# A four-stage hybrid block on one NeuronCore: loads on one queue, layer norm beside the rounds, another order in power attention

## What is computed

```python
x = x + mamba(layernorm(x))     # selective scan: E = 256 channels, 16 states
x = x + ffn(layernorm(x))       # two layers of windowed attention (8 heads of 64) and gated FFN
x = x + power(layernorm(x))     # 16 heads of 8, P = (q.k)^2 with a decay, causal
x = x + ffn(layernorm(x))       # the same weights again

# power attention, per head
log_G = cumsum(log_sigmoid(x @ Wg))
Z = 2*log(abs(S) + 1e-7) + log(scale) + log_G[t] - log_G[s], masked causal
y = exp(Z - max) @ V / sum(exp(Z - max))
```

## Time and profile before

| | |
|---|---|
| runs, median of 3 | 3021.56 us (3019.85 to 3024.13) |
| profiled execution, its own time | 3025.83 us |
| span of its trace | 3024.0 us |
| granted TensorE clock, mean | 0.975 of 2.4 GHz |
| busy: PE, DVE, ACT, POOL | 2689.8, 2430.5, 2222.0, 1390.7 us |
| first scan (L646) of Mamba | 35.63 us |
| first feed-forward | about 560 to 1497 us |
| power attention | about 1497 to 2069 us |
| second feed-forward | about 2069 to 3022 us |

### The profile page before, as it was taken

The page is one execution under the profiler, slowest core; times in us unless marked ns, Lnnn a source line. Parts: engine busy times, 40 slices in busy tenths (PEclk is TensorE's granted clock), DMA queues, the critical chain, the costliest instruction groups (busy, mean ns, idle before and its releaser), DMA issues. The chain is left out here.

```text
span 3024.0 us, 55902 instructions
## 1 busy us (share of the span) xinstructions
PE 2689.8 (89%) x18848; PEld 1827.4 (60%) x18848; DVE 2430.5 (80%) x3798; ACT 2222.0 (73%) x5986; POOL 1390.7 (46%) x1217
## 2 busy tenths in 40 slices
PE   6788988789999999999899999996899999999997
PEld 3454454356666666666677777774566666666665
DVE  7999999877777777777788888887777777777774
ACT  5688788467677677667699999994676776677674
POOL 5767777665555455545410000004555455555542
PEclk8999999899999999999999999998999999999998
DMA  3000000000000000000000000000000000000000
GB/s 93 1 1 1 1 1 1 1 1 1 2 1 1 12 13 1 1 1 1 12 13 2 2 2 2 2 2 1 1 1 1 1 1 13 16 6 5 7 7 6
DMA packets 15670, 17.83 MB, mean 6 GB/s; under 512 B 3837, under 2 KB 12862, under 8 KB 15294
## 3 DMA queue, kind: packets, MB, share of 16 engines
q1 hardware_dynamic: 13616, 12.30, 1.3%
q10 hardware_dynamic: 1774, 1.95, 0.3%
HBM read 12.16 MB, written 2.10 MB: 5 GB/s over the span
## 5 line engine op out<-in xcount | busy, mean ns | idle before, releaser
L1058 POOL TENSOR_TENSOR f_p<-f_p,f_rs 128x512 f32<-128x512 f32 (+1 forms) x256 | 321.1, 1254 | 697.9 <-DVE f_rs L1007 697.9
L901 ACT ACTIVATE f_p<-pair,f_nm 128x128 f32<-128x128 f32 (+1 forms) x1024 | 389.7, 392 | 190.0 <-DVE f_nm L996 189.3
L1050 POOL TENSOR_TENSOR f_qb<-f_kn,f_tab 128x512 f32<-128x512 f32 x256 | 441.4, 1746 | 149.6 <-DVE f_kn L975 149.6
L679 POOL TENSOR_TENSOR m_hc<-m_h,m_c 128x512 f32<-128x512 f32 x256 | 322.5, 1281 | 152.3 <-DVE m_h L646 114.0
L646 DVE TENSOR_TENSOR_SCAN m_h<-m_a,pair 128x1024 f32<-128x1024 f32 x128 | 292.2, 2283 | 11.8 <-ACT m_a L608 1.7
L855 PE MATMUL bank<-f_hnT,f_w 128*128 128x256 f32 (+1 forms) x768 | 212.6, 400 | 83.1 <-DVE f_u L1033 81.5
L608 ACT ACTIVATE m_a<-m_delta,m_A 128x255 f32<-128x255 f32 x512 | 217.3, 496 | 62.3 <-DVE m_h L646 61.7
L767 PE MATMUL pair<-f_wqkv,f_hT 128*128 128x512 f32 x512 | 253.6, 618 | 8.5 <-DVE f_kn L975 7.0
L815 PE MATMUL pair<-ident,f_p 128*128 128x128 f32 x1536 | 246.5, 284 | 14.9 <-POOL f_p L1058 6.9
L965 DVE TENSOR_REDUCE f_ss<-f_sq 128x16 f32<-128x1024 f32 x128 | 155.3, 1213 | 127.3 <-ACT f_sq L872 127.3
L533 PE MATMUL bank<-m_hc,ident 128*128 128x512 f32 x512 | 248.6, 620 | 0.0
(11 more groups left out here) (179 smaller groups left out, 6557.8 us busy)
## 6 DMA issues: line engine op xcount, KB each, us to landing
f_wqkv<-in_f_wqkv SPq DMA_DIRECT2D x4, 768.0 KB, 4.0
out_x<-X SPq DMA_DIRECT2D x16, 128.0 KB, 1.8
f_w<-in_f_w SPq DMA_DIRECT2D x4, 341.0 KB, 3.4
f_wo<-in_f_wo SPq DMA_DIRECT2D x4, 256.0 KB, 2.7
sel<-in_sel ACTq DMA_DIRECT2D x1, 768.0 KB
f_w<-in_f_w SPq DMA_DIRECT2D x4, 192.0 KB, 3.3
m_taps<-in_m_taps ACTq DMA_DIRECT2D x1, 512.0 KB, 4.9
X<-in_x SPq DMA_DIRECT2D x1, 512.0 KB, 9.1
```

Source lines behind the costliest of these rows:

```text
L679: op = nc.gpsimd.tensor_tensor(m_hc[:, g % 4, n], m_h[:, g % 2, n], m_c[:, g % 2, n].unsqueeze(1).broadcast_to([P, EC, L]), ALU.mult)
L901: op = nc.scalar.activation(f_p[:, t, j, k0:k1], SC[:, j, k0:k1], ACT.Exp, bias=f_nm[:, t, j:j + 1], accum_out=f_sm[:, t, j:j + 1])
L1050: op = nc.gpsimd.tensor_tensor(f_qb[:, t, :, o].rearrange("p (x h) d -> p x h d", x=2), f_kn[:, t, :, 32 - 32 * e:64 - 32 * e].rearrange(" ...
L1058: op = nc.gpsimd.tensor_tensor(f_p[:, t, :, k0:k1], f_p[:, t, :, k0:k1], f_rs[:, t, :].unsqueeze(2).broadcast_to([P, 4, k1 - k0]), ALU.mult)
```

## The change

1. Loads: all on SP, in this order: x of sequence 1, `m_first`, x of 2, x of 3-4, `m_last`, x of 5-8, x of 9-16, then constants and weights as before.
2. START and MF are rewritten: other places for the 16 normalisations; TensorE gets ten matmuls on a buffer of ones ahead of Mamba; `wide` is split in `wide_p` (early) and `wide_f`.
3. In the f rounds 20 to 32 and the p rounds 5 to 16, each round does the normalisation steps of one sequence for the stage after (F_BESIDE, P_BESIDE). Of the 16 in FP and PF three are left in each.
4. P_STAGES and P_ORDER: the rounds of power attention are cut at another place and the order within them is changed on TensorE, ScalarE and VectorE. FP and PF are rewritten for it; the memset qT1 stands first in FP, ahead of the multiply pn00.

```diff
 P_ORDER = {
-    "dve": "u11 pe03 r1 m11 rm11 mid pe10 u12 m12 ot0 mid2 rm12 lo pe11 kc0 u13 kc1 m13 rm13 pe12 u00 m00 rm00 pe13 "
-        "u01 m01 ot1 rm01 u02 m02 rm02 rn0 y0 pe00 u03 rn1 y1 m03 rm03 pe01 u10 m10 min pe02 lg cum rm10 hg hi "
-        "he vc",
-    "pe": "bc01 o11 s00 pT12 bc02 s01 o12 pT13 s02 bc03 o13 s03 pT00 OT0 s10 OT1 bc10 pT01 xT s11 g bc11 o00 pT02 "
-        "o01 s12 pT03 hgT bc12 v q0 o02 pT10 o03 bc13 q1 s13 pT11 k0 o10 bc00 k1",
-    "act": "ab10 e10 xTe p03 abs ab11 exp ln e11 p10 e12 ab12 qc0 p11 qc1 e13 ab13 e00 p12 e01 ab00 p13 ab01 e02 p00 "
-        "ab02 e03 ab03 p01 p02",
+    "dve": "rm10 lg cum hg pe02 he hi r1 vc u11 pe03 mid m11 mid2 rm11 u12 lo pe10 m12 ot0 rm12 pe11 kc0 u13 kc1 "
+        "m13 rm13 pe12 u00 m00 rm00 pe13 u01 ot1 m01 rm01 rn0 u02 y0 m02 u03 m03 rm02 rn1 rm03 y1 pe00 u10 m10 "
+        "pe01 min",
+    "pe": "pT03 o01 q0 o02 pT10 o03 bc13 q1 s13 pT11 k0 o10 bc00 k1 o11 bc01 s00 pT12 bc02 s01 o12 pT13 s02 bc03 o13 "
+        "s03 OT0 bc10 s10 OT1 pT00 bc11 xT s11 g pT01 o00 bc12 pT02 s12 hgT v",
+    "act": "e12 p10 ab12 qc0 p11 qc1 e13 ab13 e00 p12 e01 ab00 p13 ab01 e02 p00 ab02 e03 ab03 p01 e10 ab10 p02 xTe "
+        "e11 abs exp ab11 ln p03",
...
 START = {
+    "dve": "n1: st mv z n2: st c0: nw inc n3: st n4: st n2: mv n3: mv n2: z n4: mv n5: st n6: st n7: st n8: st n5: "
+        "mv n6: mv n7: mv n9: st n8: mv n3: z c0: skip A n4: z n5: z n10: st n9: mv c0: ones n11: st n12: st m1: ue "
+        "n6: z n10: mv n7: z n8: z n13: st n11: mv n14: st n12: mv m1: r1 delta n15: st m1: lo n16: st m1: bx0 h0 "
+        "n9: z n13: mv m2: bx1 n14: mv m2: h1 bx2 h2 bx3 h3 ue bx4 n15: mv m2: h4 bx5 h5 r1 bx6 delta h6 lo bx7 n16: "
+        "mv m2: h7 bx0 h0 m3: bx1 h1 n10: z m3: bx2 yg h2 n11: z m3: bx3 n12: z m3: h3 ue bx4 x h4 n13: z m3: bx5 h5 "
+        "r1 bx6 delta h6 lo bx7 h7 n14: z m3: bx0 n15: z m3: h0 n16: z",
...
+P_BESIDE = {"dve": [("kc0", "mv", 4), ("rm13", "z", 4), ("pe00", "st", 3)],
+            "pool": [("", "ve", 4), ("", "rs", 4), ("", "xb", 4)]}
+F_BESIDE = {"dve": [("z2", "st", 2), ("pe111", "mv", 3), ("rs11", "z", 3)],
+            "pool": [("pn10", "ve", 3), ("pn10", "rs", 3)]}
...
+def span(eng, ph, first, last, base=0, beside={}, use=0, count=0):
 
     for k in range(first, last + 1):
-        yield from window(eng, ph, k, base)
+        mine = [(at, ("n", s, use * NSEQ + k - back - count)) for at, s, back in beside.get(eng, []) if k - back > count]
+        yield from (n for at, n in mine if at == "")
+        for item in window(eng, ph, k, base):
+            yield item
+            yield from (n for at, n in mine if at == item[1])
...
+            for n, ((a, e), part) in enumerate(zip(X_PARTS, x_loaded)):
                 sp.dma_start(X[:, a:e, :].rearrange("p b (t d) -> p b t d", t=T), xv[:, a:e]).then_inc(part, 16)
+                if n == 0:
+                    for t, name in m_first:
+                        sp.dma_start(t, ins[name]).then_inc(m_first_loaded, 16)
+                if n == 2:
+                    for t, name in m_last:
+                        sp.dma_start(t, ins[name]).then_inc(m_last_loaded, 16)
...
+                if ph == "c":
+                    pe.wait_ge(small_set, SMALL)
+                    for _ in range(10):
+                        nc.tensor.matmul(pair[2][:, 0:L], ones[:, 0:P], ones[:], start=True, stop=True)
```

FP on VectorE and GpSimd begins, before and after:

```diff
-    "dve": "n1: st n2: st n3: st n4: st n1: mv n2: mv f33: nm00 pe111 n5: st n6: st f33: rs00 nm10 n1: z f33: z1 "
-        "rs10 st nm01 mv n7: st n3: mv n4: mv p1: min n8: st p1: lg cum n5: mv f33: hn n6: mv f33: rs01 n7: mv n9: "
-        "st p1: hg hi f33: pe101 nm11 n10: st n11: st n8: mv p1: he vc p2: r1 mid n12: st p2: mid2 f33: u1 u0 rs11 "
+    "dve": "f33: nm00 pe111 rs00 nm10 z1 rs10 st nm01 mv hn rs01 p1: min p2: lg cum hg f33: pe101 p2: he f33: nm11 "
+        "p2: hi r1 f33: u1 p2: vc mid mid2 n14: mv f33: u0 rs11 z2 f34: pe111 z1 p2: lo kc0 kc1 f34: st mv p2: u00 "
-    "pool": "f33: pn00 n1: ve n2: ve n1: rs n2: rs f33: vv rv pn10 pn01 zb c0: qT1 n3: ve n4: ve n3: rs n5: ve n4: "
+    "pool": "c0: qT1 f33: pn00 vv rv pn10 pn01 c0: qT0 n14: ve f33: zb pn11 f34: vv rv n15: ve f34: zb n14: rs n15: "
```

More of the change, by code:

```diff
@@ L99 @@
 P_STAGES = [
[6 rows of a table removed]
-P_ORDER = {
[7 rows of a table removed]
+    "xT xTe g abs min exp ln hgT v",
[5 rows of a table added]
+P_ORDER = {
[7 rows of a table added]
     "pool": "x"}
@@ L247, in join @@
             yield ph, token, bases.get(ph, 0) + k - (LAG[ph][token] if ph in LAG else 0)
-def span(eng, ph, first, last, base=0):
-    for k in range(first, last + 1):
-        yield from window(eng, ph, k, base)
+P_BESIDE = {"dve": [("kc0", "mv", 4), ("rm13", "z", 4), ("pe00", "st", 3)],
[3 more added lines that the diff above has]
+def span(eng, ph, first, last, base=0, beside={}, use=0, count=0):
+    for k in range(first, last + 1):
+        mine = [(at, ("n", s, use * NSEQ + k - back - count)) for at, s, back in beside.get(eng, []) if k - back > count]
[3 more added lines that the diff above has]
+            yield from (n for at, n in mine if at == item[1])
 def program(eng):
@@ L260, in program @@
     yield from join(eng, MF[eng], {"n": NSEQ})
-    yield from span(eng, "f", MF_F + 1, FP_F - 1)
+    yield from span(eng, "f", MF_F + 1, FP_F - 1, 0, F_BESIDE, 2, NSEQ)
     yield from join(eng, FP[eng], {"n": 2 * NSEQ})
-    yield from span(eng, "p", FP_P + 1, PF_P - 1)
+    yield from span(eng, "p", FP_P + 1, PF_P - 1, 0, P_BESIDE, 3)
     yield from join(eng, PF[eng], {"n": 3 * NSEQ, "f": 2 * NSEQ})
@@ L1340, in _ @@
             xv = ins["x"].rearrange("b (t p) d -> p b t d", p=P)
-            for (a, e), part in zip(X_PARTS, x_loaded):
+            for n, ((a, e), part) in enumerate(zip(X_PARTS, x_loaded)):
                 sp.dma_start(X[:, a:e, :].rearrange("p b (t d) -> p b t d", t=T), xv[:, a:e]).then_inc(part, 16)
+                if n == 0:
[4 more added lines that the diff above has]
+                        sp.dma_start(t, ins[name]).then_inc(m_last_loaded, 16)
             for t, name in consts:
@@ L1371, in step @@
             def step(ph, s, i):
-                if ph == "m":
+                if ph == "c":
+                    pe.wait_ge(small_set, SMALL)
+                    for _ in range(10):
+                        nc.tensor.matmul(pair[2][:, 0:L], ones[:, 0:P], ones[:], start=True, stop=True)
+                elif ph == "m":
                     m_pe(pe, s, i, i % 2)
@@ L1382, in _ @@
         def _(act):
-            for t, name in m_first:
-                act.dma_start(t, ins[name]).then_inc(m_first_loaded, 16)
-            for t, name in m_last:
-                act.dma_start(t, ins[name]).then_inc(m_last_loaded, 16)
             credit(act, act_m, act_f, act_p)
@@ L1450, in first @@
                     pool.wait_ge(small_set, SMALL)
-                elif s == "wide":
+                elif s == "wide_f":
                     nc.gpsimd.memset(f_hT[:, 0:1], 0.0).then_inc(wide_set, 1)
                     nc.gpsimd.memset(f_p[:], 0.0).then_inc(wide_set, 1)
+                elif s == "wide_p":
                     nc.gpsimd.memset(p_v[:, :, :, :, 0:PS + 1].rearrange("p b t h d -> p (b t) h d"),
```

## The result

| | before | after |
|---|---|---|
| median | 3021.62 us, 4 runs (3019.85 to 3024.13) | 2993.56 us, 4 runs (2993.03 to 2994.82) |
| profiled execution, its own time | 3025.83 us | 2993.73 us |
| span of its trace | 3024.0 us | 2992.0 us |
| granted TensorE clock, mean | 0.975 | 0.976 |
| busy: PE, DVE, ACT, POOL | 2689.8, 2430.5, 2222.0, 1390.7 us | 2689.7, 2435.6, 2213.8, 1397.2 us |

The ratio is 0.9907, 95% interval 0.989 to 0.9924: 28 us faster, where 2990 was forecast (range 2974 to 3012). No engine's busy time moves by more than 8.2 us (ScalarE's, down). What went is mostly waiting.

The account below looks back on a forecast made before the run. VectorE was taken to bound the first Mamba rounds, ScalarE (33.4 of 34.4 us busy) power attention's. Terms -4.3 -4 +0 +0 -6 -10 -7 sum to -31.3: 3025.8 to 2994.5, on the median 2990, range 2974 to 3012.

Parts of the forecast that it names:

- Start: Up to Mamba's first scan: loads issued from SP alone bring the scan from 35.63 to 31.3, 4.3 us less.
- 17 us by the same rates: Start: the last part of x, behind 4 MB in the queue, lands at 17 us, against 17.4 before.
- I take no loss: Start: one load queue in place of two costs nothing, as rates stay at 360 to 400 GB/s from 20 us.
- First Mamba rounds: From 36 to 132 us: fewer normalisation halves and earlier memsets save VectorE up to 6.4 us, taken as 4 less.
- Joint out of Mamba: Feed-forward joint after Mamba: all 16 normalisations still to do, so 0 (bounds -3 and +3).
- Feed-forward rounds: Thirteen rounds: the added normalisation steps fit in VectorE's waits, ending where z2 starts; 0, rounds stay at 28.00 us.
- Rival B: Feed-forward rounds: the normalisation holds GpSimd's multiply, about 0.4 us a round for 13 rounds, +5, total 2995; 11%.
- Joint into power attention: From 1468 to 1549: the early memset and 13 sequences taken out save 6 us of TensorE's 14.3 idle.
- Power attention: Rounds: the new order removes one ScalarE and one TensorE wait, 0.7 us less in each of 14 rounds, 10 us.
- Rival D: Power attention: the bank 0 chain (abs to q0) becomes the bound, +2.0 us a round, total 3028, slower; 8%.
- Joint out of power attention: Three of 16 sequences left there: 7 us less, 4.5 from statistics and aggregates, 2.5 from the first feed-forward rounds.
- VectorE 6.7 us, and 3.5 above 84: Joint out of power attention: statistics and aggregates take VectorE 6.7 us; three first feed-forward rounds take 87.5, 3.5 above 84.

Follow-up runs that it names:

- experiment 3: Changed kernel with the 13 Mamba loads issued from ScalarE again, x, constants and weights from SP, all lists as changed; 2993.62 us.
- experiment 4: Changed kernel with the memsets wide_p and wide_f back in Mamba's third round, behind GpSimd's second group product; 2996.65 us.
- experiment 7: Changed kernel with no normalisation beside the rounds, the 13 sequences back in the joints into and out of power attention; 3004.54 us.
- experiment 8: Changed kernel with the p_qT memsets late again in the joint into power attention, and 36 idle TensorE matmuls in the joint out of it; 2997.02 us.
- experiment 5: Three kernels changing only TensorE's power attention list in the kernel before: bc12 earlier 3089.22 us, pT03 later 3019.09, bc12 earlier with pT03 and o01 later 3091.84.
- pT03 alone: Kernel before with pT03 moved between v and q0 in TensorE's power attention list; 33.93 us a round in place of 34.37, 3019.09 us in all.
- the start's edit: Changed kernel with statistics and aggregate of sequence 9 and statistics of 10 to 12 moved behind ue in VectorE's start list; alone 2993.08 us.

## Why the prediction was right, point by point

**Start: right in sign, mis-sized.** The term was -4.3; the first profile shows -1.2, and the means over executions -1.6 (35.2 to 33.6), all of it from the loads, as with two issuers and the new lists the scan is at 36.06 (experiment 3). The chain that moves up moved by 3.3, the convolution by 2.8 to its start and 5.4 to its end, ue followed the last part of x as said. The step that failed is "17 us by the same rates": x landed at 19.0 to 20.6 in the seven executions that show it, 20.62 in the first profile; ue came 4.4 behind it (5 forecast) and the scan 9.45 behind ue (8.9 forecast). The rates of the earlier trace rows were those of two issuers. "I take no loss" for one queue leant on the rule that a second issuing engine saves only issue time (the Trainium skill, DMA: Bandwidth & Descriptors, "Issuing engines are not separate DMA queues"). The page calls that time "usually small relative to the DMA itself", and the runs here don't agree: with eight loads of 65 KB and less among the thirteen, x landed 1.2 to 2.8 us later than in experiment 3, of which the order of the loads may be a part. The prediction's "The trace agrees" was read from 20 us on; the dip lies at 7 to 9.

**First Mamba rounds: the size failed, by the discount.** 6.4 us of VectorE were counted, and 6.1 went (16.7 to 10.6), by luck in part: 16 halves "at 1.0 each" are 16 us and not 10.3. The records of the twenty overlap (1.08 each, 16.7 in all), and after they are 0.70 each. "The rest of the pipe was partly hiding it, so 4" was wrong: the stretch fell by 7.0. In the earlier trace rows VectorE is busy 93.0 of 96 us, which leaves 3 us to hide behind. Experiment 4 shows 2.9 of the 7.0 to be the memsets'; the rest is by the lists, and not taken apart. Start and first rounds together came to 8.2 where 8.3 were forecast, but the two errors have different causes.

**Joint out of Mamba: 0 forecast, -4.4 in the profiles.** Over four executions of the old joint and nine of the new one the means are 173.7 and 170.9, -2.9, just inside the bound of 3; the execution of before on which the sum was made is the slowest of its four here, by 2.6 to 3.5 us, which may be part of why it stood 4.3 above its median. What differs each time is the third round: 32.8 to 34.1 us before, 28.9 to 30.1 after (34.05 and 29.64 in the two profiles). Before, three normalisations stood ahead of u1 and qs1 and two, the 3.09 us of the earlier trace rows, ahead of z2, and the whole round had eight, with 7.77 us of VectorE; after, it has six, with 4.79, three of them right ahead of z2. That the places do it was not tried. The first round is 5.7 us shorter too, but starts 5.4 later behind Mamba's last sequence.

**Feed-forward rounds: right.** 28.00 with the normalisation in them, which ends where z2 starts, as the prediction had it. Rival B is out: the multiply takes 1.48 as it did. Its cited rule, a pair of ports held for the whole instruction (the Trainium skill, SBUF — State Buffer, "SBUF: two separate sides"), agrees with experiment 4, where VectorE's work ended with the last memset. There it also held across five memsets, with nothing of VectorE ending in between. In these rounds the held one is the second half of the normalisation (1.49 us by its record), not the multiply.

**Joint into power attention: right at -6.6 for -6, in part by luck.** The normalisations are worth 4.2 (experiment 7). The memsets are worth 4.4 in the changed kernel (experiment 8), but there through pn11 behind the first of them, not through a cast like the one of 4.15 us on which the term leant. In the kernel before, that cast did end 0.14 behind the memset (1486.42 and 1486.28); what it cost there was not tried, as no run moves the memset in the old lists. The two overlap, as 4.2 and 4.4 are more than 6.6, and the 6 was chosen out of 14.3 us idle. The 16 us of VectorE were too many as well: with the thirteen back in the joint it is busy for 9.1 us more (99.81 to 90.76).

**Power attention: right.** -0.73 a round over thirteen, for 0.7 in fourteen. The round closes at 33.64 (33.6 forecast), qc0 waits 0.25 (0.3). VectorE's additions cost nothing. The step that was thin is that the gain was put down to TensorE's order alone: experiment 5 shows that this order without ScalarE's and VectorE's costs 4 us a round, and that 0.44 of the 0.73 comes from pT03 alone. Rival D had something of the kind, a late chain on in-order engines; it is what happens when half of the change is made, though the late one is the copy behind bc12 there, not g.

**Joint out of power attention: the term failed.** -7 forecast, -1.8 in the profiles. Over the executions with the new joint and no fill the mean of six is 136.6, against 138.5 in the one execution with the old lists; putting the 13 sequences back costs 4.7 in one execution, 2.7 of them at a lower clock ahead of the round. The failed step is "VectorE 6.7 us, and 3.5 above 84": VectorE's busy time fell by 15.5 us over the stretch, 7.2 of them in the first feed-forward round (20.10 to 12.87), and that round became 0.95 us shorter. TensorE is busy there for 13.81 of 28.03 us, at a clock of 0.62, and ahead of its second qk waits 4.45 us for VectorE's kn: the round goes by one sequence's own chain, and the normalisations lay mostly beside it.

The sum was right to 1 us in the profiles (-31.3 for -32.0) partly because the terms' errors cancelled: +3.1 at the start, -3.0 in Mamba, -4.4 in its joint, +5.2 in the other. Against the medians, 2990 is 3.6 too hopeful.

## What to carry to other kernels

Free an engine of work only where it ends the waits: here the same thirteen normalisations are worth 4.2 us out of one joint and 1.8 to 4.7 out of the next, where a single sequence's chain runs at a low clock and the same lists differ by 5.6 us between executions. A reordering of one in-order engine has to be read with the lists of the others, since an instruction moved up waits for its tile's last reader, and everything behind it waits too. And where a joint leaves TensorE idle, look at the granted clock of the next rounds too: idle matmuls raised it here, and the kernel that has them is 7.6 us faster, with the start's edit in it.
